# Attention numbered by group over the whole batch, with three load slots, four values passes per group and the next scores in front of each pass

## The reference

```python
x = x + layernorm(attention(layernorm(x)))     # x: 4 x 1024 x 256, 16 heads of size 16, causal, latent K/V
x = x + layernorm(moe(layernorm(x)))           # 8 experts, top 2, 256 -> 1024 -> 256
# attention, per head:
q_lat = q @ k_eff                              # queries folded onto a latent of 64
attn  = softmax(where(causal, q_lat @ c_kv.T / sqrt(16), -inf))
y     = (attn @ c_kv) @ v_eff
```

## Time and profile before

| | |
|---|---|
| median of 3 runs | 1312.33 us (1309.05 to 1312.41) |
| the profiled execution's own time | 1311.21 us |
| its span | 1309.6 us |
| PE busy | 1065.6 us, 81% |
| DVE busy | 815.3 us, 62% |
| ACT busy | 640.7 us, 49% |
| POOL busy | 585.0 us, 45% |
| mean share of the 16 DMA engines | 52% |

### The profile page before, as it was taken

One profiled execution on the slowest core, in us unless ns is written; L12 is line 12 of the kernel. 1 busy time (PEld: TensorE's weight loads), 2 busy tenths in 40 slices (PEclk: granted clock), 3 DMA queues, 4 the chain that ended last, 5 costly groups with the idle time before them and its releaser, 6 DMA issues. The chain is left out here.

```text
span 1309.6 us, 24611 instructions
## 1 busy us (share of the span) xinstructions
PE 1065.6 (81%) x7457; PEld 813.6 (62%) x7457; DVE 815.3 (62%) x2300; ACT 640.7 (49%) x1111; POOL 585.0 (45%) x675
## 2 busy tenths in 40 slices
PE   5966799999999999999805430999999999999900
PEld 2533455555555555555305330999999999999900
DVE  5737577777777777776068630555565556655567
ACT  2640266666666666666726420444444444444533
POOL 4204156556556565556646773122322222222237
PEclk9986699999999999999955555999999999999955
DMA  4998657777777777632444133414433414231173
GB/s 141 374 293 151 100 136 160 160 158 159 162 159 160 160 160 158 151 103 98 163 134 165 69 127 108 165 58 163 178 108 117 169 52 181 99 122 41 49 265 128
DMA packets 94609, 190.00 MB, mean 145 GB/s; under 512 B 28244, under 2 KB 59364, under 8 KB 86276
## 3 DMA queue, kind: packets, MB, share of 16 engines
q1 hardware_dynamic: 83584, 163.19, 44.9%
q0 software_dynamic: 7680, 22.09, 4.9%
q10 hardware_dynamic: 3272, 3.84, 2.2%
HBM read 109.54 MB, written 79.02 MB: 144 GB/s over the span
## 5 line engine op out<-in xcount | busy, mean ns | idle before, releaser
L772 ACT ACTIVATE att_pt<-att_ps_s 128x1024 f32<-128x1024 f32 (+3 forms) x384 | 297.8, 815 | 186.1 <-PE att_ps_s L687 181.0
L1512 ACT ACTIVATE moe_hf<-moe_ps_h,moe_b 128x256 f32<-128x256 f32 x288 | 134.5, 474 | 225.8 <-PE moe_ps_h L1468 211.5
L797 DVE CUSTOM_DVE_ANT_0 att_ps_m<-att_ps_m,keep_future 128x384 f32<-128x384 f32 (+1 forms) x256 | 153.9, 650 | 82.9 <-PE att_ps_m L650 82.9
L650 PE MATMUL att_ps_m<-att_k,att_q 128*128 128x512 f32 (+3 forms) x576 | 183.4, 391 | 1.2 <-DVE att_pm L797 0.6
L805 DVE TENSOR_REDUCE att_pm<-att_ps_m 128x1 f32<-128x512 f32 x256 | 161.4, 684 | 22.2 <-PE att_ps_m L650 22.2
L595 POOL TENSOR_SCALAR_AFFINE_SELECT att_pt<-att_pt 128x512 f32<-128x512 f32 x128 | 81.3, 636 | 200.0 <-ACT att_pt L772 200.0
L687 PE MATMUL att_ps_s<-att_q,att_k 128*128 128x512 f32 (+3 forms) x576 | 160.2, 367 | 6.3 <-ACT att_pt L772 5.2
L1421 POOL DMA_INDIRECT ys<-moe_o,moe_home x72 | 74.1, 1029 | 185.2 <-DVE moe_o L1551 172.3
L687 PEld LDWEIGHTS att_ps_s<-att_q,att_k 128*128 128x128 f32 x576 | 93.7, 189 | 60.9 <-issue 28.9
L1545 DVE TENSOR_TENSOR moe_hTl<-moe_hf,moe_hTh 128x256 fp32r<-128x256 f32 x288 | 124.0, 431 | 9.9
L650 PEld LDWEIGHTS att_ps_m<-att_k,att_q 128*128 128x128 f32 x576 | 104.7, 197 | 36.8 <-issue 11.9
(11 more groups left out here) (200 smaller groups left out, 2570.2 us busy)
## 6 DMA issues: line engine op xcount, KB each, us to landing
att_raw<-in_w SPq DMA_DIRECT2D x16, 1024.0 KB, 6.2
ws<-att_raw_hi SPq DMA_DIRECT2D x16, 1024.0 KB, 3.9
ws<-att_raw SPq DMA_DIRECT2D x16, 1024.0 KB, 5.8
moe_rows<-xs SPq DMA_DIRECT2D x38, 258.0 KB
att_q<-qs SPq DMA_DIRECT2D x66, 128.0 KB
att_k<-ks SPq DMA_DIRECT2D x66, 128.0 KB
weights_w_0h<-ws SPq DMA_DIRECT2D x8, 1024.0 KB
weights_w_0l<-ws SPq DMA_DIRECT2D x8, 1024.0 KB
```

Of the source, the lines that this page charges most:

```text
L650: ins = pe.matmul(out[:, end - keys:end], qg[slot][:, h // 2, i * P:(i + 1) * P], kg[slot][:, h, k0:k0 + keys], start=not whole, stop=not ...
L772: act.activation(pt[:, blk % NPT, 2 * p:2 * p + 2, off:CH], ps_s[k % 2][:, :, off:CH], ACT.Exp, scale=HS ** -0.5).then_inc(ex_done, 1)
L797: return dve.tensor_tensor_reduce(src, src, future[:, CH - keys:CH], 1.0, LOWEST, ALU.add, ALU.max, pm[:, g % 2, 0, h, place:place + 1])
L1512: act.activation(hf[:, f % NHB], ps_h[f % NHB][:], ACT.Relu, bias=b1[r][:, f:f + 1]).then_inc(hf_done, 1)
```

## The change

- `NSL` goes from 4 to 3 slots, and `NPT` from 4 to 6 blocks of exponents. SP now loads group g + 2 in group g. The wait for the values of group g - 1 stands ahead of it as before, now in step 1 of the same group.
- A group's first 16 units (`AHEAD`) are dealt two groups ahead, and they start in step 13 of group g, behind its pass. The maxima are turned in step 16 instead of 17.
- Group 0's steps start right after its own 38 units, its turn and the `max_rows`; no unit of group 1 is in front of them. Group 0 has no units in steps 0 to 7 and then three per step (`DEALT_FIRST`); group 1 has 44 units (`DEALT_SECOND`).
- A group has four values passes, after steps 1 (blocks 8 to 11 of the group before), 9 (blocks 0 to 3), 13 (4, 5) and 17 (6, 7). The scores of step k + 1 stand in front of the pass of step k.
- SP loads group 2 only after `max_rows(0)` and after group 1 has landed. Two memsets of the fourth slot, one empty output turn and the empty second half of each maxima turn fall away. SP's loop is written out instead of running over registers.

The diff, cut to what decides the order:

```diff
-NSL = NG
+NSL = 3
-NPT = 4
+NPT = 6
+PASSES = {1: (-4, -3, -2, -1), 9: (0, 1, 2, 3), 13: (4, 5), 17: (6, 7)}
-DEALT = ((1, 0), (1, 2), (1, 0), (2, 0), (2, 0), (1, 0), (2, 0), (0, 0), (2, 0), (1, 3), (1, 0), (2, 0),
+AHEAD = 16
+DEALT = ((1, 0), (1, 3), (1, 0), (1, 0), (1, 0), (2, 0), (2, 0), (1, 0), (1, 0), (1, 3), (1, 0), (1, 0),
...
+DEALT_FIRST = ((0, 0),) * 8 + ((3, 0), (3, 3), (3, 0), (3, 0), (3, 0), (3, 3), (3, 0), (3, 0),
...
@@ all_jobs
+                    if units and units[0][1] <= g + 2 and not (units[0][1] == g + 2 and units[0][2] >= AHEAD):
+                        jobs.append((units.pop(0), number))
...
+                    more += [("turn", g + 1, 0)] if k == (20 if g == 0 else 16) and g + 1 < GROUPS else []
@@ block.sync
+                sp.wait_ge(slots["init"][2], 2)
+                load_ones(sp, d, slots, 2)
+                for u in range(2):
+                    sp.wait_ge(keep["stored"][u], STORES * B + 1)
+                max_rows(0)
+                sp.wait_ge(*group_in(1))
+                load_group(sp, d, slots, 2)
+                fetch_raw(0)
+                for g in range(GROUPS):
+                    if 0 < g < GROUPS - 2:
+                        sp.wait_ge(pv_done, g * NB)
+                        load_group(sp, d, slots, g + 2)
+                    if g + 1 < GROUPS:
+                        max_rows(g + 1)
+                    keep_split(g)
@@ block.tensor
+                jobs(FIRST)
+                for g, steps in enumerate(DEAL):
+                    for k, step in enumerate(steps):
+                        if k - 1 not in PASSES:
+                            scores(g, k)
+                        jobs(step.early)
+                        if k in PASSES:
+                            scores(g, k + 1)
+                            values_pass(g, k)
+                        jobs(step.late)
+                values_pass(GROUPS, 1)
```

More of the change, by code:

```diff
@@ L419, in unit_keys, with __init__, all, all_jobs @@
     return len(heads) * sum(keys for _, _, keys, _ in pieces)
-DEALT = ((1, 0), (1, 2), (1, 0), (2, 0), (2, 0), (1, 0), (2, 0), (0, 0), (2, 0), (1, 3), (1, 0), (2, 0),
[L423 to L444, removed]
+class Step:
+    def __init__(self):
+        self.early, self.late = [], []
+    def all(self):
+        return self.early + self.late
+def all_jobs():
+    first = [(("unit", 0, m), m) for m in range(NU)] + [(("turn", 0, 0), NU)]
+    number = len(first)
+    units = [("unit", g, m) for g in range(1, GROUPS) for m in range(NU)]
+    groups = []
+    for g in range(GROUPS):
+        steps = []
+        for k, (early, late) in enumerate((DEALT_FIRST, DEALT_SECOND)[g] if g < 2 else DEALT):
+            step = Step()
+            steps.append(step)
+            for jobs, count in ((step.early, early), (step.late, late)):
+                for _ in range(count):
+                    if units and units[0][1] <= g + 2 and not (units[0][1] == g + 2 and units[0][2] >= AHEAD):
+                        jobs.append((units.pop(0), number))
+                        number += 1
+                if jobs is step.early:
+                    more = [("out", g, c) for c in range(2) if k == OUT_STEPS[c] and g + c > 0]
+                    more += [("turn", g + 1, 0)] if k == (20 if g == 0 else 16) and g + 1 < GROUPS else []
+                    for job in more:
+                        jobs.append((job, number))
+                        number += 1
+        groups.append(steps)
+    assert not units
+    return first, groups, (("out", GROUPS, 0), number)
+GROUPS = B * NG
+FIRST, DEAL, LAST = all_jobs()
+NUMBER = {job: n for job, n in [*FIRST, *(j for steps in DEAL for step in steps for j in step.all())]}
 def attend(nc, d, keep, slots):
@@ L480, in attend, with made, read, group_in @@
         pm_done, nh_hi, nh_done = (s.sem(n) for n in ("pm_done", "nh_hi", "nh_done"))
[L483 to L510, removed]
+        def made(n):
+            return bank_made[n % NBK], n // NBK + 1
+        def read(n):
+            return bank_read[n % NBK], n // NBK + 1
+        def group_in(g):
+            return loaded[g % NSL], ONES + (g // NSL + 1) * LOADS
+        def rows_in(g):
+            return m_in[g % NSL], (g // NSL + 1) * 64
         with nc.Block() as block:
@@ L514, in _, with max_rows @@
             def _(sp):
[L515 to L517 removed]
+                def max_rows(g):
+                    sp.wait_ge(*read(NUMBER["turn", g, 0]))
                     slot = g % NSL
@@ new lines, in _ @@
+                pe.matmul(ps_o[:], onesb[:, 0:P], onesb[:], start=True, stop=True)
+                jobs(FIRST)
+                for g, steps in enumerate(DEAL):
+                    for k, step in enumerate(steps):
+                        if k - 1 not in PASSES:
[5 more added lines that the diff above has]
+                        jobs(step.late)
```

308 lines of the change are left out of this document (130 added, 178 removed).

## The result

The changed kernel takes 1356.97 us (median of 4 runs, 1355.53 to 1358.07) where the kernel before takes 1312.09 beside it: a ratio of 1.0349, 95% interval 1.0331 to 1.0367, 44.9 us slower. The forecast was 1320 us and its range ended at 1330.

What follows compares the result with a forecast made beforehand. PE's stream, 98% busy, was taken as the bound (period 31.82 us). Start -1.2, three slots +10.6 and tail -2 gave +7.4 on 1311.2, 1318.6 us; the shown median lies 1.1 higher: 1320 us, range 1303 to 1330.

Steps and rivals of the forecast that it cites:

- Three slots: Steady groups: the later load closes a loop of 32.7 us against 31.82, +0.9 us per group, +10.6 us over 12.
- M to F: From SP's write of a group's maxima (M) to its fetch of the next split weight (F): 9.0 us.
- first unit to M: From the load's landing, through the late units and the turn, to SP's write of the maxima: 5.1 us.
- the ring: Closed loop of maxima write, weight fetch, load landing, late units, next write; lower bound of the period, 32.7 us (31.0 to 34.4).
- Would PE be late anyway?: PE's stream from turn to behind step 13's pass: 26 to 28 us, load at 28.8, so PE waits 1 to 3.
- Four passes, scores ahead (hidden): Values passes: 8.20 us per group after 8.50, a second exponent for ACT beside each; hidden except at the end.
- The tail: Groups 14 and 15, at attention's end: less idling of ACT, net -2 us (-5 to +1).
- The start: Up to group 2's maxima write: scores start at 131 us, the 21 us gained mostly taken back; -1.2 us (-6 to +2).
- M(2): SP's write of the maxima of group 2, where the steady part begins: forecast at 208.2 us against 209.39.
- Rival 4: TensorE's granted clock falls in PE's wait for each load, 2.1 us for each of 12 waits: 1345 us, chance 0.03.
- Rival 3: Step 1's longer pass also delays the load's issue, each period 1.1 us longer: 1333 us, chance 0.10.
- Rival 5: Scores ahead wait for the exponent before last, PE stalls, only the tail's gain goes: 1323 us, within the main 0.57.

Runs made afterwards that it cites:

- six_passes_plain: The changed kernel with six passes of two blocks put back and no scores in front of a pass: 1351.3 us.
- changed_with_four_slots: The changed kernel with four slots and five buffers of exponents in place of three and six, the load a group earlier: 1352.3 us.
- three_slots_only: The kernel before with the new start and written-out code (1301.3 us), changed from four slots to three: 1441.9 us.
- four_passes_plain: The changed kernel with its four passes kept but no scores in front of a pass: 1351.6 us.
- loads_together: The written-out kernel with the old start (1290.3 us), with group 2's load asked for beside group 1's: 1304.6 us.
- loops_written_out_only: The kernel before with its work written out by number, old start, one turn job fewer, group 2's load after group 1's: 1290.3 us.

## Why the prediction was wrong

The forecast was 1320 us, and the changed kernel took 1357: +37.3 us in the steady part where I had +10.6.

- *Three slots*: in the changed kernel M to F is 9.04 us (9.0), first unit to M 5.0 (5.1), and the load ends 18.5 to 19.0 us behind F (18.6), but nobody waits for it. Where PE does wait, in six_passes_plain, the ring is 34.5 us, not 32.7. I had taken the landing as the moment when DMA activity drops, and PE starts only 0.7 us behind its end; the rest is a load that ends later and 5.45 us to M. So where the ring binds it costs 2.7 us per group against the kernel before and not 0.9; six_passes_plain took 1351 us, which is outside my range too.
- *"Would PE be late anyway?"* is the step that failed. I put PE's stream from the turn to the place behind step 13's pass at 26 to 28 us, from DVE's pace of 0.605 us per unit; it takes 419.91 to 451.07, 31.2 us. DVE is not the bound there: it is busy 20.9 us of these 31.2, so the 20 us for the units were about right and the 6 to 8 us for the passes were too few. The period of the kernel before, less the 3.8 us from the first unit to the turn in the changed kernel, is 28.0 us, the top of my range: the same work at the old order's pace. The new order adds 3.2 to that, which I had priced at nothing. So PE arrives behind the load, its stream is the period, and the wait of 1 to 3 us that I forecast isn't there. changed_with_four_slots shows it: with the ring opened the period stays at 34.92 us.
- *Four passes, scores ahead (hidden)*: the sign was wrong and the cover too. From the new start, scores ahead cost 1.2 us a group alone, four passes 0.5, the changed table 1.4; table and scores together 3.1.
- *The changed table* had no price in the sum except through the ring: it costs 19 us alone, and with the scores ahead 24 us more than these alone (1344 for 1320).
- *The tail*: -2 forecast (-5 to +1), +5.2 measured. It holds a whole group at the slow pace, and around group 15 ACT idles 8.1 us (28.00 less 19.87), where it idled 7.0 before.

```profile
670.00:698.00 28.00, 23.74 (x167) 11.00 (x169) 0.00 (x0) 19.87 (x28) 19.06 (x17) 0.95 0.39 147
```

- *The start*: first scores at 131.18 us (131), M(1) 175.8 (173.2), M(2) 211.58 (208.2): +2.2 for -1.2, 0.2 over the end of its range. That the 21 us are mostly taken back was right; by M(2) all of them are. What it hid: beside the old start, asking for group 2's load behind group 1's is worth 14 us.
- *The rivals.* Rival 4 came nearest in size (1345 us), by a mechanism that isn't in the steady part of the changed kernel; where PE waits for the load it happens, behind some waits from 2.28 us on. The wait that I priced it from the earlier trace rows was a poor witness: the granted clock was 0.50 from 122 us on, before that wait began at 123.8. In the changed kernel one wait of 2.27 us for the maxima rows of group 1 has it too:

```profile
179.77 0.73 PE L679 MATMUL att_ps_s<-att_q,att_k 128*128 128x512 f32 x2 [2.27 <-DMA att_q<-att_mt]
181.00:184.00 3.00, 3.00 (x13) 1.08 (x15) 1.74 (x5) 2.40 (x3) 0.63 (x1) 0.52 0.99 418
```

- Rival 3 saw the load issued late (433.24 us, 3.1 behind the fetch), but that load isn't awaited. Rival 5 had part of the mechanism, scores that wait for the exponent before last, and charged it to the tail alone.
- *What stays open*: how much of the 3.1 us is waiting and how much is matmuls that last longer in the trace. PE's busy time rose too, 31.3 to 32.8 us a group for the same work; the records don't separate a matmul held back from one at work. Why table and scores ahead cost more together than apart was not tried beyond moving the units. That the waits of PE's scores for ACT and of its units for DVE are what lengthens the period is read from the traces, not shown by a run that removes them.

## What to carry to other kernels

When one engine is busy 98% in the trace, take its old period as the first estimate of its new stream; an estimate from another engine's pace is a lower bound only. A reordering can add waits on that engine: each of the three tried here alone (table, scores ahead, four passes) did, 0.5 to 1.4 us a group. Price each reordering as if no transfer bound it, and each transfer as if no order did, and expect the larger; here these were 34.9 and 34.5 us. Take a transfer's end from an instruction that waits for it, not from the DMA engines going quiet. When a transfer is the first thing waited for, look at what runs beside it: here holding back the later load was worth more than all that was reordered.

## What the hardware showed

- In three_slots_only the granted clock was down to 0.50 within a wait of 8.50 us for a load, and the first 128x512 bf16 matmul behind it lasted 0.58 us in place of 0.38. In four_passes_plain a wait of 2.28 us had the fall only behind it: that matmul still took 0.38 us, and the stretch from 452.3 us had 0.53. Waits of 2.71 us (four_passes_plain) and 3.15 us (six_passes_plain) had no fall at all.
- In six_passes_plain the matmul that waited for a load started 0.6 to 0.7 us behind the last DMA activity, in all 12 groups.
- Two loads asked for side by side (loads_together) made PE wait 13.95 us for the first; with the second behind the first (loops_written_out_only) PE did not wait for it, and the time was 14 us shorter.
